# Edge weights of the last stage from split half-precision rows of the radial net, in a graph network on one core

## What is computed

```python
h = relu(layernorm(x)); x = x + L0_gnn_ref(h, edge_index, ...)   # two GCN layers + projection
h = relu(layernorm(x)); x = x + L1_gnn_ref(h, edge_attr_4, edge_attr_8, edge_index, ...)
# in L1_gnn_ref:
h = edge_feats                                                    # 100000 x 8
for W in (W_mlp1, W_mlp2, W_mlp3):                                # radial net, 64 hidden
    h = SILU_2MOM * silu(h @ W / sqrt(W.shape[0]))
tpw = h @ W_mlp4 / sqrt(64)                                       # edge weights, 4 x 128 an edge
w1, w2, w3, w4 = split(tpw, 4)
p1 = w1 * s0 * y0;  p2 = (w2 * s0) * y1;  p3 = w3 * s1 * y0;  p4 = w4 * (s1 . y1) / sqrt(3)
# summed by receiver, multiplied by W_out0 and W_out1
```

## Time and profile before

| | us |
|---|---|
| median of 3 runs | 6342.22 |
| lowest, highest of them | 6321.91, 6348.5 |
| span of the profiled execution | 6349.4 |
| start and norm stage | 0 to 477 |
| layer 0 | 477 to about 2200 |
| layer 1 | about 2200 to about 3830 |
| last stage | about 3880 to the end |

### The profile page before, as it was taken

How to read it: one execution, slowest core, us unless ns; L and a number is a source line. 1 busy time by engine, 2 the same in 40 slices (tenths; PEclk the granted TensorE clock), 3 DMA queues, 4 the chain that set the end, 5 groups by cost and what they waited for, 6 DMA issues and landing times.

```text
span 6349.4 us, 121231 instructions
## 1 busy us (share of the span) xinstructions
PE 4859.7 (77%) x17030; PEld 2220.3 (35%) x17031; DVE 3249.5 (51%) x9687; ACT 2434.2 (38%) x6372; POOL 2797.3 (44%) x3192
## 2 busy tenths in 40 slices
PE   2104677888888655778888788999999999999998
PEld 1001223333333212233333334444444444444444
DVE  7761133333334312333333334777777777777676
ACT  0340022333334300111211124666666666666665
POOL 0246665554444366655444442444444333333332
PEclk9997778898989767888888888999999999999999
DMA  2126666666555466666655553444444444444433
GB/s 75 67 95 174 175 183 184 192 183 182 173 171 168 144 172 175 186 186 196 184 177 168 162 161 105 119 118 114 118 120 119 114 117 115 118 116 115 114 114 100
DMA packets 420669, 915.73 MB, mean 144 GB/s; under 512 B 62887, under 2 KB 170663, under 8 KB 420504
## 3 DMA queue, kind: packets, MB, share of 16 engines
q0 software_dynamic: 211200, 692.23, 38.3%
q1 hardware_dynamic: 209432, 223.12, 11.1%
HBM read 812.38 MB, written 102.72 MB: 144 GB/s over the span
## 4 chain that ended last, share of the span: by engine, by line
issue 31%; PE 16%; SPq 15%; DVE 11%; ACT 7%; DVEq 7%; ACTq 5%; DMA 3%; another core or an unknown queue 2%; POOL 2%; POOLq 1%; PEldq 0%
PE bank L1187 4%; PE bank L1090 4%; SPq L242 3%; DVEq L953 3%; SPq L377 3%; ACT dense_w L672 2%; ACT hB L661 2%; DMA ring<-tab_d,idx 2%; PE bank L1069 2%; ACTq L658 2%; DVE hA L961 2%; DVEq L963 2%; DVE hA L947 2%; SPq L381 1%
## 5 line engine op out<-in xcount | busy, mean ns | idle before, releaser
L489 POOL DMA_INDIRECT ring<-tab_d,idx x1760 | 1716.4, 975 | 1623.7 <-DVE ohp L863 761.3
L1069 PE MATMUL bank<-ring,ohp 128*128 x3520 | 1175.0, 487 | 1095.1 <-SPq L382 609.8
L1187 PE MATMUL bank<-dense_w,oh 128*128 128x512 f32 x3520 | 1622.0, 603 | 65.7 <-DVE dense_w L970 65.0
L489 POOL DMA_INDIRECT ring<-up_d,idx x880 | 881.2, 1001 | 496.9 <-POOL idx L485 348.6
L672 ACT ACTIVATE dense_w<-hA,hC 128x128 f32<-128x128 f32 x2640 | 819.6, 389 | 653.4 <-DVE hA L961 599.9
L1069 PEld LDWEIGHTS bank<-ring,ohp 128*128 x3520 | 398.0, 113 | 1854.3 <-issue 1705.5
L1187 PEld LDWEIGHTS bank<-dense_w,oh 128*128 128x128 f32 x3520 | 634.0, 190 | 859.0 <-issue 672.8
L861 DVE COPY idx<-src_i x880 | 162.8, 185 | 1239.0 <-issue 551.7
L1090 PE MATMUL bank<-dense_w,AT 128*128 128x512 f32 x1568 | 689.0, 592 | 0.0
L485 POOL COPY idx<-src_i 128x2 int32 x440 | 81.1, 184 | 1046.8 <-DVE dense_w L970 967.0
L1177 PE MATMUL bank<-w,hC 64*128 64x256 f32 x3520 | 503.8, 405 | 32.6 <-issue 21.8
(11 more groups left out here) (150 smaller groups left out, 4478.7 us busy)
## 6 DMA issues: line engine op xcount, KB each, us to landing
ring<-tab_d,idx POOLq DMA_INDIRECT x1760
hC<-hid_d SPq DMA_DIRECT2D x440, 64.0 KB
tab_d<-tout SPq DMA_DIRECT2D x98, 256.0 KB, 2.1
tw<-tab_d SPq DMA_DIRECT2D x98, 256.0 KB
hid_d<-hC SPq DMA_DIRECT2D x98, 256.0 KB
ring<-up_d,idx POOLq DMA_INDIRECT x880
r_d<-r SPq DMA_DIRECT2D x49, 256.0 KB
r0w<-r_d SPq DMA_DIRECT2D x49, 256.0 KB
```

The source lines that it names most:

```text
L489: g_.indirect_dma_start(ring_v[:, b, k, :], None, table, bass.IndirectOffsetOnAxis(idx_t[:, b, k:k + 1], 0)).then_inc(S["got"][b % len(S[" ...
L1069: ins = pe.matmul(bank[0][:, :], ohp_k[:, bass.ds(at + k, 1), :].rearrange("p b n -> p (b n)"), ring_k[:, bass.ds((at + k) * 2 + h, 1), :] ...
L1187: ins = pe.matmul(bank[h][:, :], oh[:, b, k, :], msg[:, b, k, h, :], start=False, stop=False, skip_group_check=True)
```

## The change

Three places change.

In the last stage `hid` is half-precision and has 128 rows: the high parts of the 64 hidden rows on the first 64, the low parts on the others. `w4` is split likewise, into `w4h` and `w4l`, each standing on both halves of the rows. A pair's edge weights are then, for each of two tiles and two halves of the columns, a matmul with `w4h` and one with `w4l` that adds to it.

In layer 0 `act3` is followed by a multiplication on ScalarE into `hH` (rounded to half), and VectorE makes `hL`, what is left, in a new step `hidden_low`. SP stores both in 8 DMAs per window, in a place of its list ahead of the load of the self rows. `act3` waits for `hidden_low` of the window before instead of for the store.

At the start the scale of the split is worked out: the largest edge feature (`ef_all`, all of them, loaded once for that), the largest of `w4`, and column sums of the absolute values of the other radial weights, spread over the rows by five matmuls with ones. A few small tiles move to borrowed memory.

```diff
-        hid_d = dram("hid_d", (NG, P, P))
+        hid_d = dram("hid_d", (NG, P, 2 * P), F16)
...
-        hid = hC[:, 0, 0:256].rearrange("p (b n) -> p b n", b=2)
+        hid = hC[:, 0, 0:256].bitcast(F16).rearrange("p (b n) -> p b n", b=2)
+        ef_all = dense_w[:, 1:5, :, :].rearrange("p a c n -> p (a c n)")[:, 0:2 * RB * NG]
...
-            for k in W:
-                sp.dma_start(W[k][:, :, :], a[k].rearrange("(c p) n -> p c n", p=P)).then_inc(s_big, 16)
+            sp.dma_start(ef_all, a["ef_t"].rearrange("r (q n) -> (r q) n", q=8)).then_inc(p_ef, 16)
+            sp.dma_start(W["W0"][:, :, :], a["W0"].rearrange("(c p) n -> p c n", p=P)).then_inc(s_big, 16)
...
+            sp.wait_ge(p_efm, 1)
+            for k in ("lw0", "W1", "lw1", "pw"):
+                sp.dma_start(W[k][:, :, :], a[k].rearrange("(c p) n -> p c n", p=P)).then_inc(s_big, 16)
...
-                        sp.wait_ge(a3, j * 2 + 1 + b)
-                        sp.dma_start(hid_d[bass.ds((j * 2 + b) * 4, 4), :, :].rearrange("g p e -> p g e"),
-                                     hC[:, b, :].rearrange("p (g e) -> p g e", g=4)).then_inc(hid_out[b], 16)
+                        sp.wait_ge(h_lo, j * 2 + 1 + b)
+                        for k in range(2):
+                            for i, t in enumerate((hH, hL)):
+                                sp.dma_start(hid_d[bass.ds((j * 2 + b) * 4, 4), i * HID:(i + 1) * HID,
+                                                   k * P:(k + 1) * P].rearrange("g p e -> p g e"),
+                                             t[k * HID:(k + 1) * HID, b, :].rearrange("p (g e) -> p g e", g=4)
+                                             ).then_inc(hid_out[b], 16)
...
-                    peeled(sp, [(0, relay), (0, load_ef), (0, self_rows), (4, store_hid), (3, store_r), (3, store_tab)])
+                    peeled(sp, [(0, relay), (0, load_ef), (4, store_hid), (0, self_rows), (3, store_r), (3, store_tab)])
...
+            ac.wait_ge(p_scale, 1)
+            ac.mul(w4h[:, :], w4[:, :], bound[:, 3, 6:7]).then_inc(p_w4h, 1)
+            ac.mul(wo[:, :, :], wo[:, :, :], peak[:, 10:11])
...
                 def act3(j):
                     for b in range(2):
-                        after(ac, hid_out[b], j, 16)
+                        if not isinstance(j, int) or j > 0:
+                            ac.wait_ge(h_lo, j * 2 - 1 + b)
                         ac.wait_ge(m3, j * 2 + 1 + b)
                         ac.activation(hC[:, b, :], bank[4 + b][:, :], ACT.Silu).then_inc(a3, 1)
+                    for b in range(2):
+                        after(ac, hid_out[b], j, 64)
+                        ac.wait_ge(a3, j * 2 + 1 + b)
+                        ac.mul(hH[:, b, :], hC[:, b, :], bound[:, 2, 6:7]).then_inc(h_hi, 1)
...
+            ve.wait_ge(p_ef, 16)
+            ve.tensor_reduce(peak[:, 0:1], ef_all, X, ALU.max, apply_absolute_value=True).then_inc(p_efm, 1)
+            ve.wait_ge(s_wsc, 1)
+            ve.tensor_reduce(peak[:, 1:2], w4[:, :], X, ALU.max, apply_absolute_value=True)
+            ve.drain()
+            for i in range(2):
+                ve.tensor_scalar(diag[:, i, :], ident[:, :], peak[:, i:i + 1], None, ALU.mult).then_inc(p_diag, 1)
...
+            ve.wait_ge(p_sum, 1)
+            ve.tensor_reduce(peak[:, 2:4], bank[0][:, 0:2 * P].rearrange("p (i n) -> p i n", i=2), X, ALU.max)
+            ve.tensor_reduce(peak[:, 4:7], bank[1][:, 0:3 * P].rearrange("p (i n) -> p i n", i=3), X, ALU.max)
...
+            power_of_two(2)
+            power_of_two(3)
...
+            ve.wait_ge(p_w4h, 1)
+            ve.scalar_tensor_tensor(out=w4l[:, :], in0=w4[:, :], scalar=bound[:, 3, 6:7], in1=w4h[:, :],
+                                    op0=ALU.mult, op1=ALU.subtract)
...
+                def hidden_low(j):
+
+                    for b in range(2):
+                        ve.wait_ge(h_hi, j * 2 + 1 + b)
+                        ve.scalar_tensor_tensor(out=hL[:, b, :], in0=hC[:, b, :], scalar=bound[:, 2, 6:7],
+                                                in1=hH[:, b, :], op0=ALU.mult, op1=ALU.subtract).then_inc(h_lo, 1)
+
...
-                    peeled(ve, [(0, onehots), (2, copy_at), (1, self_rows), (3, add_bias), (3, second_norm)])
+                    peeled(ve, [(0, onehots), (4, hidden_low), (2, copy_at), (1, self_rows), (3, add_bias),
+                                (3, second_norm)])
...
-                        ins = pe.matmul(w_bank[k][h][:, 0:2 * P], hid[k * HID:(k + 1) * HID, b, :],
-                                        w4[k * HID:(k + 1) * HID, h * 2 * P:(h + 1) * 2 * P], start=True, stop=True)
+                        o, at = w_bank[k][h][:, 0:2 * P], slice(h * 2 * P, (h + 1) * 2 * P)
+                        pe.matmul(o, hid[:, b, k * P:(k + 1) * P], w4h[:, at], start=True, stop=False)
+                        ins = pe.matmul(o, hid[:, b, k * P:(k + 1) * P], w4l[:, at], start=False, stop=True)
```

More of the change, by code:

```diff
@@ L87, in build @@
         rse = sb("rse", [P, 2, NW])
-        bound = sb("bound", [P, 2, 8])
+        bound = sb("bound", [P, 4, 8])
+        peak = sb("peak", [P, 12])
         dense_w = sb("dense_w", [P, 5, KC, D])
@@ L95, in build @@
         w4 = sb("w4", [P, D])
+        w4h = sb("w4h", [P, D], F16)
+        w4l = sb("w4l", [P, D], F16)
         wo = sb("wo", [P, 4, P])
@@ L126, in build @@
         hC = sb("hC", [P, 2, D])
+        hH = sb("hH", [P, 2, D], F16)
+        hL = sb("hL", [P, 2, D], F16)
         xin = sb("xin", [P, 2, D])
@@ L447, in _ @@
             g_.memset(zeros[:, :], 0.0).then_inc(s_cst, 1)
+            g_.memset(ones[:, :], 1.0).then_inc(s_cst, 1)
             g_.memset(w1[:, :], 0.0).then_inc(s_wz, 1)
@@ L723, in _ @@
             ve.tensor_copy(lo_f[:, :], lo_i[:, :])
-            ve.wait_ge(s_cst, 6)
+            ve.wait_ge(s_cst, 7)
             ve.tensor_copy(iota[:, :], iota_i[:, :])
@@ L756, in _, with power_of_two @@
             ve.tensor_copy(rcol_i[:, :], rcol[:, 0:2]).then_inc(s_rcol, 1)
+            def power_of_two(i):
+                ve.drain()
+                ve.tensor_scalar(bound[:, i, 3:4], bound[:, i, 2:3], 1e-30, None, ALU.max)
+                ve.drain()
+                ve.tensor_scalar(bound[:, i, 4:5].bitcast(I32), bound[:, i, 3:4].bitcast(I32), 0x7F800000, None,
+                                 ALU.bitwise_and)
+                ve.drain()
+                ve.tensor_scalar(bound[:, i, 5:6], bound[:, i, 4:5], 2.0 ** -14, None, ALU.mult)
+                ve.drain()
+                ve.reciprocal(bound[:, i, 6:7], bound[:, i, 5:6])
             for L in range(2):
@@ L1046, in _ @@
             touch(bank[6][:, 0:NW], NW, False).then_inc(deg_sum, 1)
+            pe.wait_ge(p_diag, 2)
+            pe.wait_ge(p_abs, 3)
+            for i in range(2):
+                pe.matmul(bank[0][:, i * P:(i + 1) * P], ones[:, :], diag[:, i, :], start=True, stop=True)
+            for i, n in enumerate((2 * RB, P, P)):
+                ins = pe.matmul(bank[1][:, i * P:(i + 1) * P], ones[0:n, :], absw[0:n, i, :], start=True, stop=True)
+            ins.then_inc(p_sum, 1)
             pe.wait_ge(s_big, 16 * len(W))
+            pe.wait_ge(p_scale, 1)
             pe.wait_ge(deg_ready, 1)
```

52 lines of the change are left out of this document (31 added, 21 removed).

## The result

| | before | after |
|---|---|---|
| median, us | 6339.11 (4 runs) | 6471.93 (4 runs) |
| lowest, highest | 6321.91, 6348.5 | 6467.12, 6477.27 |
| ratio, 95% interval | | 1.0218 [1.0198, 1.0237] |
| span of the profiled execution | 6349.4 | 6475.5 |

The median before is that of the three runs above and one more. The change is 2.2% slower; 1.3% was forecast (6426 us), and 6471.93 lies in the range. The mechanisms held, their sizes not all of them, and most of the loss turned out to hang on the sort of chip, as the experiments show.

The account below looks back on a forecast made before the run. The prediction took a ScalarE-VectorE ring to bound the last stage and a POOL, SP, TensorE, VectorE loop the graph layers. Terms 0 - 8 + 0 + 82 + 10 = +84 us gave 6426 us, range 6335 to 6620.

Parts of the forecast that it names:

- The bound of the last stage: Last stage: ScalarE and VectorE hand pairs back and forth every 4.93 us; TensorE, though busy 466 of 500 us, isn't the bound.
- Part 1, the edge weights: Last stage: eight half-precision matmuls replace four fp32 ones per pair; TensorE's gain of about 0.1 us becomes waiting, 0 us.
- Rival 3: Last stage: TensorE is the bound after all, the shorter group saves 88 us, time 6256 with rival 1; chance 0.07.
- the fourth rival: Last stage: weight loads don't hide, eight matmuls take 1.76 us, 189 us more in all, 6615 with the rest; chance 0.06.
- Part 2, the splitting: Layer 0: ScalarE's and VectorE's added multiplications fit into their waits, 0 us for both, at most 132 us.
- The term of -8 us: Layer 0: act3's wait for the earlier window's stores, 20.9 us in total, goes away ahead of TensorE's first radial layer.
- Part 3, SP's stores: Layer 0: six more stores per window on SP delay what queues behind them, +82 us, bounds 0 and 182.
- The later windows: Layer 0's other 37 windows: a third of SP's free price for six stores, 1.3 us each, 48 us.
- rival 2: Layer 0: stores beside gathers cost SP up to 2.2 us each and every delay shows, some +300 us, 6642; chance 0.12.
- Rival 1: Layer 0: SP's stores stay hidden under TensorE's window work everywhere, leaving +10 - 8, 6344 us; chance 0.17.
- The DMA pieces: Layer 0: 1024 more pieces per window, 2.9 us of DMA time on engines busy some 60%, 0 on top.
- Part 4, the start: Start: a maximum over edge features and small operations added, less waiting for ext, +10 us, from 6 to 18.

Follow-up runs that it names:

- the second pair of traces: The kernel before and the change, both unchanged, run again on another chip with slow SP instructions: 6312.64 and 6457.42 us, ratio 1.0218.
- the opened ring with fp32 weights: Kernel before with ScalarE's q0 a pair ahead and zero matmuls at window ends in the last stage, fp32 weights, no splitting: 5814.32 us, ratio 0.9804.
- the filled one: The change plus eight zero matmuls ahead of TensorE's wait for the copied sums at the last stage's window ends: 5951.09 us, ratio 1.0044 to the kernel before.

## Why the prediction was right, point by point

**The bound of the last stage** was read rightly. The ring between ScalarE and VectorE set 4.93 us: opened, it gave 4.69 with fp32 weights, which is TensorE's own time. That half of the argument, that a faster TensorE would bring nothing, is shown from both sides, by the unchanged period in the change and by the 0.38 us that appear when the ring is open.

**Part 1, the edge weights: 0, by right reasoning from a wrong size.** The eight matmuls at 0.107 us came out at 0.88 / 8 = 0.11. But the saving was put at 0.04 to 0.2 us a pair and is 0.38. The mis-sized term compared the groups' busy times, 1.13 and 1.03, which both hold the tail of the last matmul; start to start it is 1.07 against 0.88. And it left out the two changes between 64 and 128 rows, 0.20 us a pair. Rival 3 would so have been priced at 0.38 x 440 = 167 us, not 88 (with the ring open, half precision took 115 + 20 = 135 us off the last stage); what kept it from coming true is the ring, not its size. Of the weight loads the prediction asked whether they hide. They do: the loads, 100 ns each on average, lie beside the matmuls, and the 1.76 us of the fourth rival did not come.

```profile
L1257 PEld LDWEIGHTS bank<-w4l,hC 128*128 128x128 f16 x1760 | 176.0, 100 | 24.4 <-issue 2.8
```

TensorE: Matmul & The Clock Gate in the Trainium skill divides the number of columns by 1.2 to get a load's ns (section LDWEIGHTS), by estimate 107 for such a load, near the 100 measured. The prediction held against that, eight loads in 0.38 us, but each of those is recorded with 102 to 123 ns; they overlap one another. Its 1.76 us add a load's whole time to each matmul's. The page's section "Step-by-step: what each phase is for" has the next load pulled ahead beside a running matmul, and the trace agrees.

**What part 1 missed: +20 us at the windows' ends.** The prediction followed the saved time to the wait ahead of each sum and no further. TensorE, earlier done with its group and its sum, also waits longer for the copied sums, by half a microsecond: 107.0 us in 46 waits, 2.33 each, where it was 88.8 in 48, 1.85 each. Some 0.3 of the 0.5 us are the shorter group and sum (4.3 us from the group's start to the sum's end where it was 4.6); the rest was not traced. In 19 to 24 of 49 window ends (four kernels with the half-precision weights and without filler) the clock then was at 1.2 GHz for at least a part of the transposes; with the shorter wait that was so in 1 or 2. Eight matmuls of zeros in the wait took the loss back entirely: 2156.9 us against 2176.9. The Trainium skill describes waits that send the clock down again and again (TensorE: Matmul & The Clock Gate, section on HAM oscillation). The trace agrees that the clock falls again and again, with 22 of 49; the page's example waits for a DMA, TensorE here for VectorE's copy.

**Part 2, the splitting: 0 forecast,** +3 (slow SP) and +1 to +5 us (without) measured in layer 0. VectorE's work went into the wait that was named: ahead of L875, now L936, it fell from 167.1 to 86.5 us. (Of the 167.1 only 100.8 were for ScalarE, 2.1 us a window and not 3.5; 1.5 us still fit.) The term of -8 us for the wait that leaves act3 can't be seen: the wait for the stores reappears ahead of ScalarE's high parts, 143.0 us in layer 0, where it was 20.9 ahead of act3. It hid there.

```profile
ACT hH L663 <- DMA hid_d<-hL: 143.0, 51, 6.9
```

**Part 3, SP's stores.** Forecast +82, measured +119 (+117 in the second pair of traces). The large windows came in at 37.1 us for 34, and that is in part luck. The 0.7 us for a DMA was the difference between the layers, put down to two DMAs a window. In the second trace of the kernel before, the large and the later windows differ between the layers by 4.0 and 17.5 us and not by 11.3 and 5.2. These are its rows for layer 1, against 293.53 and 953.53 in layer 0:

```profile
2563.12:2852.69 289.57, 115.23 (x340) 38.81 (x340) 0.82 0.62 187
2852.69:3788.69 936.00, 277.96 (x900) 97.49 (x900) 0.91 0.59 178
```

By these rows the same working gives 12 us for the large windows. On chips without slow SP instructions the layers differ by 9 to 11 and by 75 to 83 us with two stores or with eight of 512 bytes, and yet six more stores cost 1 to 4. So the difference between the layers isn't the price of their DMAs. What the large windows paid on a chip with slow instructions is 21 us for the count and 16 for the shape (291.8, 313.0, 329.4), and the shape had no term.

The later windows are the mis-sized term, 48 against 81.7. It took SP to run free there, as in the earlier trace rows at 1538 us, and charged a third of 4.05 us a window. SP did not run free there. From the start of a window's first store to the end of its last, the eight took 9.6 us on average (5 to 13), where the two had taken 1.4: 8.2 us more. SP's timeline of one such window, 12.9 us from the first store to the end of the last:

```profile
1673.92 0.67 SPq L412 DMA_DIRECT2D hid_d<-hH  x1
...
1686.10 0.71 SPq L412 DMA_DIRECT2D hid_d<-hL  x1
```

Of the 9.6 us the new shape makes 6.3, which is what eight such stores took in every large and nearly every later window of the kernel with 256-byte pieces on a chip without slow instructions; the slow instructions make the rest. Of the 8.2 us more, 81.7 / 37 = 2.2 us showed. The mechanism of rival 2, slow stores in most windows, was thus at work; what it had wrong is that each delay shows. The bounds (0 to 182 us) held the result.

What the prediction could not see is that the earlier trace rows's slow price belongs to the chip: with the two stores of the old shape on a chip without slow SP instructions (the opened ring with fp32 weights) no window took more than 1.1 us for them, beside gathers or not. On such chips everything together cost layer 0 24 us, and the change would come to a ratio near 1.008, an estimate from the filled one's 1.0044 and the last stage's 20 us. Rival 1, in which SP's tail stays hidden, is nearly what such a chip shows, with 512-byte pieces to within 4 us.

**The DMA pieces: 0 forecast, right.** In layer 0 the queue carried 122912 packets in 14.7% of 16 engines over 1473 us, 28 ns each, against 45 ns in the earlier trace rows: a packet holds 58% of the bytes on average and takes 63% of the time.

```profile
q1 hardware_dynamic: 122912, 63.35, 14.7%
```

DMA: Bandwidth & Descriptors (the Trainium skill, Specifications) has transfers below 512 bytes read, changed and written back. No such price shows: in the two kernels that differ in the pieces alone, twice as many pieces for the stores took 317 us more of 900 x 16. Whether the 20 us that the smaller shape costs without slow SP instructions come from SP's longer issue (2.1 us a window more) or from the pieces' landing, the runs don't separate; 45 x 2.1 = 95 us of longer issue would be enough for it.

**Part 4, the start: +10 forecast, +10.5 measured** at the norm stage's first statistics, 6.67 for the maximum, 12.71 instead of 16.29 us of waiting for ext. At the first transposes of layer 0 it was +14.6 us in the first pair of traces, +8.5 in the second, and 7 to 10 on chips without slow SP instructions.

**The sum** of +84 us was low by the later windows' stores and by the windows' ends of the last stage, which had no term; the medians differ by 133.

**What stays open:** +7 us between layer 0's last transposes and layer 1's first, in every kernel with the splitting on chips without slow instructions (249.5 and 250.7 us against 242.5 to 244.8), +7.5 and +1.1 in the two pairs with them. No run was made for it. "It would be wrong if layer 1 moved" was too strict a test: it moves by 37 us between executions and chips.

## What to carry to other kernels

When a step off the critical path gets shorter, follow its idle time to every place where that engine waits, and look whether its clock falls there; then ask whether the ring that holds it off the path can be opened, since only that turns the gain into time (here 2 and 3.7% instead of a loss of 2.2%). Count what a queue's instructions cost in number and in shape, and keep a change of data layout from multiplying them: parts stored side by side in one tile left in the two transfers of before. A cost read from one chip's issuing engine may belong to that chip: look at the longest time of an instruction that does nothing. And a difference between two stretches of one trace is a price only if a second trace of the same kernel shows it again; here 11.3 and 5.2 us became 4.0 and 17.5.

## What was not expected of the hardware

Two sorts of chips run the same program 6.6 to 7.1% apart (5922 and 6313 to 6342 us), and the difference lies in the gather layers and the start: the last stage's 48 windows take 2157 us on both. On the slower sort some 13% of SP's register and semaphore instructions take about 0.7 us, on the other none. That these cause the layers' whole difference is not shown.

A DMA issue of 64 rows by 4 groups of 256 bytes takes SP 0.60 us at the median, one of 128 rows by 512 bytes 0.33, for the same 64 KB.

A segment sum of the same eight instructions takes 3.63 us between groups of fp32 matmuls on 64 rows and 3.43 between groups of half-precision ones on 128, 0.1 us for each change of the number of rows.
